# An own written order for the first four rounds of a software pipeline: a hybrid of convolution, attention and expert layers on one core

## The chip, the cores and the metric

The kernel runs on one NeuronCore of one Trainium2 chip. Its engines run side by side, each through its own list of instructions in order: TensorE (PE, matrix products into the eight PSUM banks), VectorE (DVE), ScalarE (ACT), GpSimd (POOL) and SyncE (SP, here only the issuer of loads and stores). They wait for each other through semaphores. The metric is the device time of one execution in microseconds (us), lower is better.

## The reference, cut to what matters

A batch of 16 images of 128 channels by 16 x 16 places goes through a dynamic convolution, an attention layer and a layer of eight experts. Only the first of these is touched in the rounds that the change rewrites; the other two follow it in the same pipeline.

```python
g = _gn(x)                                # mean and variance over groups of 4 channels of an image
key = softmax(K_w @ g + K_b)              # 49 rows of 256 places for each image
filters = g @ key.T                       # 128 channels x 49 taps
filters = conv0_w @ filters + conv0_b
filters = (filters - mean) * rsqrt(var + eps) * ln_w + ln_b
filters = conv1_w @ relu(filters) + conv1_b
x = x + depthwise_conv(g, filters)        # 7 x 7, an own filter for each image and channel
t = to_tokens(x)
t = t + attention(layernorm(t))           # softmax(tanh tanh'), 256 tokens of an image
t = t + experts(layernorm(t))             # 8 experts, the best 2 of each token
```

## The kernel before, in words

The 16 images are worked on as eight pairs. A loop over rounds, `for i in range(rounds)`, stands once in the list of each engine; in round `i` the pair `i` is in stage n (group normalisation), pair `i - 1` in stage a (keys and raw filter), `i - 2` in stage b (filter and spectrum), `i - 3` in stage c (product in the spectrum and inverse), `i - 4` in d (attention) and later pairs further on (`stages`). So round 0 has stage n alone, round 1 n and a, and so on: the first four rounds fill the pipeline. The order inside a round is that in which the loop's body is written on each engine, the same body for full rounds and for those that are mostly empty.

- Stage n of pair n. DVE: `bn_stats` and `bn_aggr` of the image (`gn_raw`, `gn_mv`). PE: the averages over groups by the constant matrix `group_avg` (`gn_avg`, line L1294), into `bank_d1`. DVE: deviation, square, sum (`gn_dev`, L955; `gn_sq`; `gn_e2`). PE: a second average (L1307). DVE: `gn_var`. POOL: power -1/2 (`gn_rstd`). DVE: `gn_bias` (L985). ACT: the normalised image `gbuf` (L627), which raises `g_done`.
- Stage a. PE waits for `g_done`, then four transposes of `gbuf` (L1215) and the key products (L1220). DVE: maximum `kmax` (L900) and shift (L907, L910). ACT: `kexp` (L589). DVE: `krec`. ACT: `kprob` (L596). PE: transposes of `kprob` (L1288), and after ACT's copies `gt` and `pt` the raw filter (L1314).
- Stage b. PE: first convolution (L1156), mean (L1160), spectrum of the image (L1106), mean square (L1164), second convolution (L1169). Stage c. PE: spectrum of the filter (L1174); DVE: products into `zhat`; PE: inverse (`image`, L1189, into `bank_o`).
- Beside this, in rounds 1 to 8, the weights of one expert are multiplied out (`expert_weights`, PE L1199 into `bank_d0`; DVE `weight_bias` L686 and `low_part` L692, ACT `w_high`).
- `keep_busy(bank, count)` (PE L1101) issues `count` products whose result nobody reads; they stand at places where PE would otherwise wait. In rounds 0 to 4 there are 25 of them.

All constant matrices lie in one tile `const`, identity first, the averaging matrix second. PE's first instruction waits for `ld_c1` at 32, that is for the first four matrices and for `small`, which SP loads behind the first pair of images. `load_x(p)` loads pair p; SP issues pair 2 and later ones once `g_done` frees the buffer, between the reloads of the expert weights.

Of the kernel before, what the change touches and what calls it, by code (L numbers as in the profile page):

```python
# [74 lines left out]
def constants():  # L75
# [33 lines left out]
    return {"ident": ident, "group": group, "mean": mean, "before": before,  # L109
# [3 lines left out]
WIDTHS = {"ident": P, "group": P, "mean": P, "before": P, "fwd": CHUNKS * (2 * WIDE + BOTH),  # L113
# [13 lines left out]
def build(nc, a_in, out):  # L127
# [9 lines left out]
    with ctx:  # L137
# [123 lines left out]
        ld_c1 = sem("ld_c1")  # L261
# [77 lines left out]
        CC = 3  # L339

# [6 lines left out]
        def expert_in(i):  # L347
            return experts_through(i) - 1 if i in expert_rounds else None

# [5 lines left out]
        with nc.Block() as block:  # L355

            @block.sync
            def _(sp):
# [13 lines left out]
                sp.dma_start(const[:, 0:STARTS["fwd"]], a_in["const"][:, 0:STARTS["fwd"]]).then_inc(ld_c1, 16)  # L372
# [37 lines left out]
            def _(pool):  # L410
# [23 lines left out]
                for i in range(rounds):  # L434
# [3 lines left out]
                    if b is not None:  # L438
                        pool.wait_ge(fvar_done, b + 1)
                        pool.tensor_tensor(frstd[:, :], fvar[:, :], minus_half[:, 0:2], ALU.pow).then_inc(frstd_done, 1)  # L440
                    if f is not None:
                        dispatch(f, range(TILES // 2, TILES))
                    if n is not None:
                        pool.wait_ge(gn_var_done, n + 1)
                        after(pool, g_done, n - 1)
                        pool.tensor_tensor(gn_rstd[:, n % 2, :], gn_var[:, :], minus_half[:, 0:2], ALU.pow).then_inc(gn_rstd_done, 1)  # L446
                    if c is not None:
                        pool.wait_ge(ln_var_done, c + 1)
                        after(pool, z_done, c)
                        pool.tensor_tensor(ln_rstd[:, :], ln_var[:, :], minus_half[:, :], ALU.pow).then_inc(ln_rstd_done, 1)  # L450
# [9 lines left out]

                def image_power(c):
                    pool.wait_ge(ln_var_done, c + 1)
                    pool.wait_ge(z_done, c)
                    pool.tensor_tensor(ln_rstd[:, :], ln_var[:, :], minus_half[:, :], ALU.pow).then_inc(ln_rstd_done, 1)
# [11 lines left out]
                pool.wait_ge(fvar_done, PAIRS)  # L476
                pool.tensor_tensor(frstd[:, :], fvar[:, :], minus_half[:, 0:2], ALU.pow).then_inc(frstd_done, 1)
# [26 lines left out]
            def _(act):  # L504
                act.dma_start(b1c[:, :], a_in["b1c"]).then_inc(ld_bias, 16)
# [6 lines left out]
                act.wait_ge(ld_c1, 32)  # L512
# [55 lines left out]
                for i in range(rounds):  # L568
                    n, a, b, c, d, e, _ = stages(i)
                    x = expert_in(i)  # L570
                    if a is not None:

                        act.wait_ge(gt_psum, a + 1)
                        after(act, fraw_psum, a - 1)
                        after(act, ghat_psum, 2 * (a - 1))
                        act.activation(gt[:, a % 2, :, :].rearrange("p h c -> p (h c)"), bank_t[:, :], ACT.Copy).then_inc(gt_done, 1)
# [8 lines left out]
                    if a is not None:  # L585

                        act.wait_ge(kshift_done, a + 1)
                        after(act, kprob_done, a)
                        act.activation(kexp[:, :], bank_k[:, 0:HW], ACT.Exp, bias=kshift[:, 0:1], accum_out=ktot[:, 0:1]).then_inc(kexp_done, 1)  # L589
# [3 lines left out]
                    if a is not None:  # L593
                        act.wait_ge(krec_done, a + 1)
                        after(act, pt_psum, a)
                        act.activation(kprob[:, :], kexp[:, :], ACT.Copy, scale=krec[:, 0:1]).then_inc(kprob_done, 1)  # L596
                    if x is not None and b is None and a is not None:

                        act.wait_ge(wbias_done, x + 1)
                        act.activation(w_high[:, x * 2 * HID:(x + 1) * 2 * HID], bank_d0[:, :], ACT.Copy).then_inc(whigh_done, 1)  # L600
# [5 lines left out]
                    if a is not None:  # L606

                        act.wait_ge(pt_psum, a + 1)
                        after(act, fraw_psum, a)
                        act.activation(pt[:, :, :].rearrange("p h k -> p (h k)"), bank_k[:, HW:2 * HW], ACT.Copy).then_inc(pt_done, 1)  # L610
                    if x is not None and b is not None and a is not None:

                        act.wait_ge(wbias_done, x + 1)
                        act.activation(w_high[:, x * 2 * HID:(x + 1) * 2 * HID], bank_d0[:, :], ACT.Copy).then_inc(whigh_done, 1)
                    if a is not None:

                        act.wait_ge(fraw_psum, a + 1)
                        after(act, conv0_psum, a - 1)
                        act.activation(fraw[:, a % 2, :, :], bank_k[:, 0:2 * KKP].rearrange("p (s k) -> p s k", s=2)[:, :, 0:KK],
                                       ACT.Copy).then_inc(fraw_done, 1)  # L620
                    if n is not None:

                        act.wait_ge(gn_bias_done, n + 1)
# [31 lines left out]
            def _(dve):  # L655
# [227 lines left out]
                for i in range(rounds):  # L883
# [41 lines left out]
                    if n is not None and i != 1:  # L925
                        image_statistics(n)
# [964 lines left out]
```

## Time and profile before

| | |
|---|---|
| median of 3 runs | 331.99 us (330.51 to 332.82) |
| the profiled execution | 332.61 us |
| its span, first to last instruction | 330.6 us |
| PE busy in the span | 294.9 us (89%) |
| granted clock of PE, mean | 0.974 |

Times in the trace count from the first instruction of the span; the execution's own time is 2.0 us longer. PE's busy time counts the products of `keep_busy` as well. A product of fp32 operands shows in the trace as two matmul records, a transpose as one, and the end of a record is modelled, so that lengths below are taken from one group's start to the next group's start.

### The profile page before, as it was taken

The page shows a single profiled execution, that of the slowest core. Times are in us where ns is not written, and L with a number is a line of the kernel's source. Part 1 is how long each engine was busy: PE and PEld are TensorE (multiplying, and loading weights), DVE is VectorE, ACT ScalarE, POOL GpSimd, SP SyncE. Part 2 cuts the span into 40 slices and gives each one's busy share as a digit, 9 for nine tenths or more (in the row PEclk, how much of TensorE's full clock was granted, in tenths as well). Part 3 has the DMA queues.
Part 4 walks back from the last instruction along what each step waited for, and adds up shares of the span by engine and source line. Part 5 has one row for each costly group of instructions (what it writes and reads, how often), then busy time and mean ns, then how long its engine had stood idle before and what let it go on. Part 6 is the DMA issues. An engine that isn't in the chain of part 4 may idle for free.

```text
span 330.6 us, 7149 instructions
## 1 busy us (share of the span) xinstructions
PE 294.9 (89%) x1739; PEld 237.7 (72%) x1739; DVE 231.7 (70%) x1012; ACT 144.2 (44%) x465; POOL 164.8 (50%) x187
## 2 busy tenths in 40 slices
PE   0889999999999999999998988996999999999910
PEld 0557677788777787778876765885888888888810
DVE  1524374679788797877889796784776677776883
ACT  1244343625337252371520324662666666666600
POOL 3000002021163656636747775775677777676650
PEclk9979999999999999999999999997999999999985
DMA  7751423050211810001101113433333234325946
GB/s 206 261 175 29 149 70 108 0 161 14 82 48 29 287 44 25 25 18 42 34 25 50 43 41 92 107 113 95 105 98 102 83 100 114 97 79 149 332 160 249
DMA packets 29919, 33.39 MB, mean 101 GB/s; under 512 B 5064, under 2 KB 23836, under 8 KB 29626
## 3 DMA queue, kind: packets, MB, share of 16 engines
q1 hardware_dynamic: 24608, 23.64, 24.3%
q0 software_dynamic: 4352, 8.60, 7.6%
q10 hardware_dynamic: 922, 0.71, 0.6%
q8 instruction: 16, 0.26, 0.3%
q14 instruction: 21, 0.17, 0.2%
HBM read 21.69 MB, written 11.68 MB: 101 GB/s over the span
## 4 chain that ended last, share of the span: by engine, by line
PE 63%; DVE 10%; issue 7%; SPq 6%; DMA 5%; POOL 5%; ACT 2%; DVEq 0%; POOLq 0%; ACTq 0%
PE bank L1821 7%; PE bank L1189 6%; PE bank L1106 6%; PE bank L1199 4%; PE bank L1801 4%; PE bank L1796 4%; PE bank L1797 4%; PE bank L1810 4%; PE bank L1174 3%; PE bank L1181 3%; POOL rows_dram L429 3%; PE bank L1101 3%; SPq L1560 2%; SPq L1557 2%; PE bank L1791 2%
## 5 line engine op out<-in xcount | busy, mean ns | idle before, releaser
L1505 POOL DMA_INDIRECT moe_dram<-ys,xs x71 | 70.0, 987 | 28.7 <-issue 18.8
L429 POOL DMA_INDIRECT rows_dram<-row,slot x56 | 55.7, 994 | 24.6 <-issue 13.5
L1821 PE MATMUL bank<-w_all,gatedt 128*128 x284 | 44.1, 278 | 0.1
L1593 ACT ACTIVATE silu<-bank 128x256 f32<-128x256 f32 x71 | 27.3, 384 | 31.6 <-PE bank L1801 31.6
L1736 DVE SCALAR_TENSOR_TENSOR ys<-b_all,xs,bank 128x128 f32<-128x128 f32 x71 | 24.7, 348 | 22.6 <-issue 20.7
L1753 DVE SCALAR_TENSOR_TENSOR gated<-bank,xs,silu 128x256 f32<-128x256 f32 x71 | 34.3, 482 | 7.1 <-ACT silu L1593 2.7
L1821 PEld LDWEIGHTS bank<-w_all,gatedt 128*128 128x128 f32 x284 | 37.7, 193 | 0.3 <-issue 0.3
L1796 PE MATMUL bank<-w_high,x_high 128*128 x71 | 34.4, 485 | 0.7 <-ACT x_high L1580 0.7
L440 POOL TENSOR_TENSOR frstd<-fvar,minus_half 128x2 f32<-128x2 f32 x7 | 5.0, 707 | 52.4 <-DVE fvar L812 52.4
L1189 PE MATMUL bank<-zhat,const 121*128 121x256 f32 (+1 forms) x128 | 29.6, 383 | 0.1
L1801 PE MATMUL bank<-w_high,x_low 128*128 x71 | 28.9, 407 | 0.2
L1797 PE MATMUL bank<-w_low,x_high 128*128 x71 | 28.1, 396 | 0.0
L1810 PE MATMUL bank<-const,gated 128*128 128x128 f32 x142 | 27.4, 275 | 0.6 <-DVE gated L1753 0.6
L1584 ACT ACTIVATE gatedt<-bank 128x256 f32<-128x256 f32 x71 | 26.8, 378 | 1.2 <-PE bank L1810 1.1
L1810 PEld LDWEIGHTS bank<-const,gated 128*128 128x128 f32 x142 | 19.7, 141 | 9.5 <-DVE gated L1753 1.4
L1189 PEld LDWEIGHTS bank<-zhat,const 121*128 121x128 f32 (+1 forms) x128 | 23.6, 189 | 3.7 <-issue 0.5
L1580 ACT ACTIVATE x_high<-bank 128x128 fp32r<-128x128 f32 x71 | 19.7, 278 | 13.0 <-PE bank L1791 6.0
L1101 PE MATMUL bank<-const 128*128 128x256 f32 x88 | 25.2, 416 | 0.0
L1727 DVE TENSOR_TENSOR x_low<-bank,x_high 128x128 fp32r<-128x128 f32 x71 | 20.1, 283 | 5.1 <-ACT x_high L1580 4.9
L1106 PE MATMUL bank<-gt,const 128*121 128x256 f32 (+1 forms) x96 | 22.8, 385 | 0.0
L1791 PE MATMUL bank<-const,xs 128*128 128x128 f32 x71 | 19.6, 278 | 3.0 <-DMA xs<-rows_dram 2.9
L446 POOL TENSOR_TENSOR gn_rstd<-gn_var,minus_half 128x2 f32<-128x2 f32 x8 | 5.7, 715 | 32.5 <-DVE gn_var L976 32.4
(203 smaller groups left out, 617.1 us busy)
## 6 DMA issues: line engine op xcount, KB each, us to landing
xs<-rows_dram SPq DMA_DIRECT2D x71, 66.0 KB, 1.9
xc<-in_x SPq DMA_DIRECT2D x8, 256.0 KB, 2.8
wgv<-in_wg SPq DMA_DIRECT2D x8, 256.0 KB, 2.8
wgv<-in_wv SPq DMA_DIRECT2D x8, 256.0 KB, 3.1
xt<-in_xt SPq DMA_DIRECT2D x4, 512.0 KB, 4.7
xt<-moe_dram SPq DMA_DIRECT2D x8, 256.0 KB, 4.2
moe_dram<-ys,xs POOLq DMA_INDIRECT x71, 2.4
const<-in_const SPq DMA_DIRECT2D x1, 1123.0 KB, 9.1
```

Of the source, the lines that this page charges most:

```text
L429: pool.indirect_dma_start(rows_dram, bass.IndirectOffsetOnAxis(ap=slot[:, f % 2, 2 * t + k:2 * t + k + 1], axis=0), row[:, f % 2, t, k, :] ...
L1101: pe.matmul(bank, ident, const[:, 0:2 * P], start=True, stop=True)
L1106: last = pe.matmul(bank_s[r // 2][0:tile_rows[r], r % 2 * 2 * C:(r % 2 + 1) * 2 * C], fwd[:, h, tile_cols[r]], gt[:, b % 2, h, :], start=( ...
L1189: last = pe.matmul(bank_o[:, h * 2 * C:(h + 1) * 2 * C], inv[0:tile_rows[r], r, h * P:(h + 1) * P], zhat[0:tile_rows[r], r, :], start=(r = ...
L1505: pool.indirect_dma_start(moe_dram, bass.IndirectOffsetOnAxis(ap=xs[:, u, C + 1:C + 2].bitcast(U32), axis=0), ys[:, u, :], None, bounds_ch ...
L1593: act.activation(silu[:, j % 2, :], bank_h[j % 2][:, 0:HID], ACT.Silu).then_inc(S["silu_done"], 1)
L1753: dve.scalar_tensor_tensor(gated[:, j % 2, :], bank_h[j % 2][:, HID:2 * HID], xs[:, j % U, C:C + 1], silu[:, j % 2, :], ALU.mult, ALU.mult ...
L1796: pe.matmul(bank_h[j % 2][:, :], x_high[:, j % 2, :], w_high[:, bass.ds(e * (2 * HID), 2 * HID)], start=True, stop=False)
L1797: pe.matmul(bank_h[j % 2][:, :], x_high[:, j % 2, :], w_low[:, bass.ds(e * (2 * HID), 2 * HID)], start=False, stop=False)
L1801: pe.matmul(bank_h[j % 2][:, :], x_low[:, j % 2, :], w_high[:, bass.ds(e * (2 * HID), 2 * HID)], start=False, stop=True).then_inc(S["h_psu ...
L1810: last = pe.transpose(bank_g[:, h * P:(h + 1) * P], gated[:, j % 2, h * P:(h + 1) * P], ident)
L1821: last = pe.matmul(bank_y[j % 2][:, 0:C], gatedt[:, j % 2, h * P:(h + 1) * P], w2_all[:, bass.ds(e * (2 * C) + h * C, C)], start=(h == 0), ...
```

## The change

The first four rounds are no longer run by the loop. Each engine has them written out as a list of calls (`HEAD = 4`; the loops begin at `HEAD`), and the bodies of the loop become small functions that the lists and the loop share. In the lists, on PE, DVE, ACT and POOL alike, the statistics of the next pair stand earlier: `image_statistics(n + 1)` and `group_statistics(n + 1)` behind the bias of pair n, the first average right behind the key products, the deviation right behind the key shift, the second average in the middle of the round. For these four pairs the averages go to `bank_o` and not to `bank_d1` (`group_places`). The averaging matrix comes first in `const` and is loaded by itself, from ACT's queue (`ld_group`); PE starts with it and waits for the other constants after the first pair's averages. `router_weights` (the router's constants) moves from round 1 to round 3. Of the 25 products of `keep_busy` four are left.

```diff
-    return {"ident": ident, "group": group, "mean": mean, "before": before,
+    return {"group": group, "ident": ident, "mean": mean, "before": before,
...
+        def group_places(n):
+
+            return bank_o if n < HEAD else bank_d1, slice(0, 2), slice(4, 6)
...
                 load_x(0)
-                sp.dma_start(const[:, 0:STARTS["fwd"]], a_in["const"][:, 0:STARTS["fwd"]]).then_inc(ld_c1, 16)
+                sp.dma_start(const[:, P:STARTS["fwd"]], a_in["const"][:, P:STARTS["fwd"]]).then_inc(ld_c1, 16)
...
             def _(act):
+                act.dma_start(const[:, 0:P], a_in["const"][:, 0:P]).then_inc(ld_group, 16)
                 act.dma_start(b1c[:, :], a_in["b1c"]).then_inc(ld_bias, 16)
...
+                image_copy(1)
+                first_conv(0)
+                key_exp(1)
+                key_prob(1)
+                wide_spectrum(0)
+                squares(0)
+                rest_spectrum(0)
+                key_copy(1)
+                normalised_image(2)
+                filter_copy(1)
+                expert_copy(1)
...
+                group_power(0)
+                group_power(1)
+                group_power(2)
+                filter_power(0)
+                group_power(3)
+                filter_power(1)
+                image_power(0)
...
+                image_statistics(0)
+                group_statistics(0)
+                group_deviation(0)
+                group_moment(0)
+                group_variance(0)
+                image_statistics(1)
+                group_statistics(1)
+                group_bias(0)
+                bias_columns()
+                weight_differences(0)
...
+                key_max(1)
+                key_shift(1)
+                group_deviation(2)
+                group_moment(2)
+                key_reciprocal(1)
+                centred(0)
+                scaled(0)
+                group_variance(2)
...
-                pe.wait_ge(ld_c1, 32)
-
...
+                pe.wait_ge(ld_group, 16)
+                group_mean(0)
+                group_square(0)
+                pe.wait_ge(ld_c1, 32)
+                pe.wait_ge(ld_bias, 32)
+                pe.transpose(bank_b[0:EXPERTS * 4, 0:P], bgv[:, :], ident).then_inc(bgt_psum, 1)
+                keep_busy(bank_t[:, 0:2 * P], 2)
+
+                image_transpose(0)
+                keys(0)
+                pe.wait_ge(gn_var_done, 1)
+                group_mean(1)
+                expert_weights(1, 0)
+                group_square(1)
+                key_transpose(0)
+                keep_busy(bank_d1[:, 0:2 * P], 1)
+                raw_filter(0)
+                keep_busy(bank_t[:, 0:2 * P], 1)
+
+                image_transpose(1)
...
+                image_transpose(2)
+                keys(2)
+                pe.wait_ge(filt_done, 1)
+                first_conv(1)
+                pe.wait_ge(gn_var_done, 3)
+                group_mean(3)
+                pe.wait_ge(wlow_done, 2)
+                filter_spectrum(0, 0)
+                filter_spectrum(0, 1)
+                filter_mean(1)
+                group_square(3)
+                pe.wait_ge(ghat_done, 2)
+                features_spectrum(1, (0, 1))
+                key_transpose(2)
+                features_spectrum(1, (2,))
+                filter_square(1)
+                expert_weights(3, 2)
+                pe.wait_ge(gn_var_done, 4)
+                image(0)
+                raw_filter(2)
+                filter_of(1)
+
+                for i in range(HEAD, rounds):
...
-                        if a < 4:
-                            keep_busy(bank_t[:, 0:2 * P], (3, 2, 2, 4)[a])
...
-                        if b < 2:
-                            keep_busy(bank_o[:, 0:2 * P], 3)
...
-                        if c is None:
-                            keep_busy(bank_o[:, 0:2 * P], (0, 1, 5)[i])
```

What this does to the order is seen at three places. In the rows below `bank7` is `bank_d1`, `bank3` is `bank_o`, and `x4` is four equal instructions in a row.

PE at the start, before: the first product needs all that `ld_c1` counts; three idle products stand ahead of the first transposes.

```order
L1294 MATMUL bank7<-gn_mv,const 128x2
L1307 MATMUL bank7<-gn_e2,const 128x2
L1326 MATMUL bank2<-const,bgv 32x128
L1101 MATMUL bank1<-const 128x256 x3
L1215 MATMUL bank1<-const,gbuf 128x128 x4
L1220 MATMUL bank0<-gbuf,small 64x256 x2
```

PE at the start, now.

```order
L1384 MATMUL bank3<-gn_mv,const 128x2
L1389 MATMUL bank3<-gn_e2,const 128x2
L1396 MATMUL bank2<-const,bgv 32x128
L1250 MATMUL bank1<-const 128x256 x2
L1356 MATMUL bank1<-const,gbuf 128x128 x4
L1363 MATMUL bank0<-gbuf,small 64x256 x2
L1384 MATMUL bank3<-gn_mv,const 128x2
L1348 MATMUL bank6<-wgv,w1d 128x512 x2
L1389 MATMUL bank3<-gn_e2,const 128x2
```

The first two products no longer share a wait with the rest, and the averages of pair 1 (the second L1384 and L1389) now stand right behind the first pair's keys.

PE from the expert weights of round 2 to the transposes of pair 2, before: both averages of the next pair stand behind the round's long products.

```order
L1199 MATMUL bank6<-wgv,w1d 128x512 x2
L1288 MATMUL bank0<-const,kprob 128x128 x2
L1294 MATMUL bank7<-gn_mv,const 128x2
L1101 MATMUL bank3<-const 128x256 x5
L1307 MATMUL bank7<-gn_e2,const 128x2
L1314 MATMUL bank0<-pt,gt 128x64 x4
L1169 MATMUL bank2<-small,frelu 49x128 x2
L1101 MATMUL bank1<-const 128x256 x2
L1215 MATMUL bank1<-const,gbuf 128x128 x4
```

PE from the first average of pair 2 to the transposes of pair 2, now.

```order
L1384 MATMUL bank3<-gn_mv,const 128x2
L1255 MATMUL bank4<-gt,const 121x256 x4
L1309 MATMUL bank2<-fsum,const 128x2
L1389 MATMUL bank3<-gn_e2,const 128x2
L1255 MATMUL bank5<-gt,const 124x256 x2
L1369 MATMUL bank0<-const,kprob 128x128 x2
L1313 MATMUL bank2<-fsqs,const 128x2
L1348 MATMUL bank6<-wgv,w1d 128x512 x2
L1377 MATMUL bank0<-pt,gt 128x64 x4
L1318 MATMUL bank2<-small,frelu 49x128 x2
L1356 MATMUL bank1<-const,gbuf 128x128 x4
```

The first average stands ahead of the spectrum, the second ahead of the spectrum's last part, the key transposes and the weights, and no idle product is left between them.

DVE in the same round, before: the deviation `gn_dev` of the next pair stands behind the two long steps on the expert weights.

```order
L812 TENSOR_SCALAR fvar<-bank2 128x2
L686 TENSOR_TENSOR bank6<-bank6,bg_row 1x512
L692 TENSOR_TENSOR w_low<-bank6,w_high 128x512
L955 TENSOR_TENSOR gn_dev<-gn_mv,bank7 128x2
L956 COPY gn_mean<-bank7 128x2
L958 TENSOR_TENSOR gn_sq<-gn_dev 128x2
L963 TENSOR_TENSOR gn_e2<-gn_sq,gn_mv 128x2
L818 SCALAR_TENSOR_TENSOR fln<-flw,frstd,small 128x49 x2
L823 TENSOR_SCALAR frelu<-fln 128x98
L976 TENSOR_SCALAR gn_var<-bank7 128x2
L985 SCALAR_TENSOR_TENSOR gn_bias<-gn_mean,gn_rstd 128x2
```

DVE in the same round, now.

```order
L947 TENSOR_REDUCE kmax<-bank0 128x1
L951 TENSOR_TENSOR ksum_b<-kmax,small 128x1
L954 TENSOR_TENSOR kshift<-small,ksum_b 128x1
L969 TENSOR_TENSOR gn_dev<-gn_mv,bank3 128x2
L970 COPY gn_mean<-bank3 128x2
L972 TENSOR_TENSOR gn_sq<-gn_dev 128x2
L976 TENSOR_TENSOR gn_e2<-gn_sq,gn_mv 128x2
L958 RECIPROCAL krec<-ktot 128x1
L866 TENSOR_TENSOR fcen<-f0,bank2 128x98
L870 TENSOR_TENSOR flw<-fcen,small 128x98
L982 TENSOR_SCALAR gn_var<-bank3 128x2
L874 TENSOR_SCALAR fvar<-bank2 128x2
```

The four short steps on the groups moved from behind the weights to right behind the key shift.

## Rows read from the trace of the kernel before

**Rows 1.** Windows of round 3, of round 4, and of a stretch in round 1.

```profile
core 0: us, PE busy (x) PEld busy (x) DVE busy (x) ACT busy (x) POOL busy (x), PEclk, DMA share, GB/s
36.62:53.82 17.20, 17.20 (x86) 13.30 (x86) 9.84 (x40) 5.99 (x19) 2.40 (x3) 1.00 0.29 88
53.82:72.68 18.86, 18.26 (x102) 14.37 (x101) 10.92 (x46) 8.04 (x28) 2.40 (x3) 1.00 0.25 77
19.80:23.10 3.30, 3.30 (x14) 2.18 (x12) 0.57 (x3) 1.77 (x4) 0.17 (x1) 0.50 0.49 162
```

**Rows 2.** Timeline of PE at the start: start, length, line, records, wait before.

```profile
7.59 0.59 PE L1294 MATMUL bank<-gn_mv,const 128*128 128x2 f32 x2 [7.59 <-DMA small<-in_small]
9.44 2.77 PE L1101 MATMUL bank<-const 128*128 128x256 f32 x6
12.00 1.06 PE L1215 MATMUL bank<-const,gbuf 128*128 128x128 f32 x4
12.99 0.65 PE L1220 MATMUL bank<-gbuf,small 128*64 128x256 f32 x4
```

**Rows 3.** Timeline of PE in round 3, from the transposes of pair 2.

```profile
36.62 0.65 PE L1215 MATMUL bank<-const,gbuf 128*128 128x128 f32 x4
...
37.79 0.46 PE L1156 MATMUL bank<-fraw,small 128*128 128x98 f32 x2
38.19 1.99 PE L1174 MATMUL bank<-filt,const 49*121 49x256 f32 x8
40.10 0.38 PE L1160 MATMUL bank<-fsum,const 128*128 128x2 f32 x2
40.34 2.83 PE L1106 MATMUL bank<-gt,const 128*121 128x256 f32 x12
43.01 1.46 PE L1101 MATMUL bank<-const 128*128 128x256 f32 x6
44.31 0.28 PE L1164 MATMUL bank<-fsqs,const 128*128 128x2 f32 x2
44.45 1.96 PE L1199 MATMUL bank<-wgv,w1d 128*128 128x512 f32 x4
46.25 0.38 PE L1288 MATMUL bank<-const,kprob 128*128 128x128 f32 x2
...
46.61 3.71 PE L1189 MATMUL bank<-zhat,const 121*128 121x256 f32 x16
50.15 0.28 PE L1307 MATMUL bank<-gn_e,const 128*128 128x2 f32 x2
...
51.31 0.64 PE L1169 MATMUL bank<-small,frelu 128*49 128x128 f32 x4
51.88 1.99 PE L1101 MATMUL bank<-const 128*128 128x256 f32 x8
```

**Rows 4.** Timeline of DVE: the first pair's statistics, steps of rounds 2 and 3.

```profile
3.73 0.75 DVE L880 BATCH_NORM_STATS2 gn_raw<-xc 128x6 f32<-128x256 f32 x2 [2.72 <-DMA xc<-in_x]
4.52 0.25 DVE L939 BATCH_NORM_AGGREGATE gn_mv<-gn_raw 128x2 f32<-128x6 f32 x2
...
32.96 0.15 DVE L955 TENSOR_TENSOR gn_dev<-gn_mv,bank 128x2 f32<-128x2 f32 x1
...
40.69 0.42 DVE L900 TENSOR_REDUCE kmax<-bank 128x1 f32<-128x256 f32 x1
```

**Rows 5.** Timeline of ACT in rounds 2 and 3.

```profile
35.48 1.09 ACT L627 ACTIVATE gbuf<-xc,gn_bias,gn_rstd 128x256 f32<-128x256 f32 x2 [0.31 <-DVE gn_bias L985]
...
43.95 0.46 ACT L589 ACTIVATE kexp<-bank,kshift 128x256 f32<-128x256 f32 x1
...
44.73 0.51 ACT L596 ACTIVATE kprob<-kexp,krec 128x256 f32<-128x256 f32 x1 [0.23 <-DVE krec L922]
```

**Rows 6.** Load of pair 1, issued at 2.2 us: the tile's view in that stretch.

```profile
L360 SPq DMA_DIRECT2D xc<-in_x x1: 434/434/434, 2.2 to 2.2; - x1
...
DMA to landing us min/median/max: 6.3/6.3/6.3
```

More of the change, by code:

```diff
@@ new lines, in normalised_image @@
+                def normalised_image(n):
+                    act.wait_ge(gn_bias_done, n + 1)
+                    after(act, keys_done, n - 1)
+                    after(act, gt_psum, n - 1)
+                    for s in range(2):
+                        last = act.activation(gbuf[:, n % 2, s * HW:(s + 1) * HW], xc[:, n % 2, s * HW:(s + 1) * HW], ACT.Identity,
+                                              scale=gn_rstd[:, n % 2, s:s + 1], bias=gn_bias[:, n % 2, s:s + 1])
+                    last.then_inc(g_done, 1)
@@ L593, in _ @@
                     if a is not None:
[L594 to L600, printed above, removed]
+                        key_prob(a)
                     if d is not None:
@@ L606, in _ @@
                     if a is not None:
[L608 to L614, printed above, removed]
+                        key_copy(a)
+                    if x is not None and a is not None:
+                        expert_copy(x)
                     if a is not None:
[L617 to L620, printed above, removed]
+                        filter_copy(a)
                     if n is not None:
[L623 to L629 removed]
+                        normalised_image(n)
                 first_conv(7)
@@ new lines, in _ @@
+                filter_variance(0)
+                group_bias(2)
+                normalised(0)
+                rectified(0)
+                weight_bias(1)
+                image_statistics(3)
+                group_statistics(3)
+                filter_of(0)
+                low_part(1)
+                weight_differences(2)
+                key_max(2)
+                key_shift(2)
+                group_deviation(3)
+                group_moment(3)
+                products(0)
+                key_reciprocal(2)
@@ new lines, in _ @@
+                centred(1)
+                scaled(1)
+                spectrum(0)
+                group_variance(3)
+                rest_products(0)
+                filter_variance(1)
+                group_bias(3)
+                normalised(1)
+                rectified(1)
+                weight_bias(2)
+                router_weights()
+                low_part(2)
+                image_sum(0)
+                image_stats(0)
+                filter_of(1)
+                z_of(0)
+                weight_differences(3)
@@ L1200, in expert_weights, with image_transpose @@
                     last.then_inc(wmul_psum, 1)
-                for i in range(rounds):
+                def image_transpose(a):
+                    after(pe, gt_done, a)
+                    pe.wait_ge(g_done, a + 1)
+                    for h in range(CHUNKS):
+                        for s in range(2):
+                            last = pe.transpose(bank_t[:, h * 2 * C + s * C:h * 2 * C + (s + 1) * C],
+                                                gbuf[:, a % 2, s * HW + h * P:s * HW + (h + 1) * P], ident)
+                    last.then_inc(gt_psum, 1)
@@ new lines, in keys, with key_transpose @@
+                def keys(a):
+                    after(pe, fraw_done, a)
+                    for s in range(2):
+                        last = pe.matmul(bank_k[s * KKP:(s + 1) * KKP, 0:HW], kw_t, gbuf[:, a % 2, s * HW:(s + 1) * HW], start=True, stop=True)
+                    last.then_inc(keys_done, 1)
+                def key_transpose(a):
+                    pe.wait_ge(kprob_done, a + 1)
+                    for h in range(CHUNKS):
+                        last = pe.transpose(bank_k[:, HW + h * P:HW + (h + 1) * P], kprob[:, h * P:(h + 1) * P], ident)
+                    last.then_inc(pt_psum, 1)
@@ new lines, in _ @@
+                filter_spectrum(0, 1)
[10 more added lines that the diff above has]
+                raw_filter(2)
+                filter_of(1)
+                for i in range(HEAD, rounds):
```

289 lines of the change are left out of this document (175 added, 114 removed).

## The prediction

> **What bounds the kernel now.** I looked first at the busy shares (TensorE 89% of the span), then at windows cut at the transposes that open each round, then at PE's timeline inside one such window. In rounds 3 and 4 PE is busy 17.20 of 17.20 us and 18.26 of 18.86 us [rows 1], so PE's list sets the pace and the other engines have room (DVE 9.84 and 10.92). But a full PE is not a useful PE: inside round 3 the six records at 43.01 and the eight at 51.88 are idle products [rows 3], 1.30 us to the square at 44.31 and 1.94 us to the transposes at 53.82 that open the next window [rows 1]. They stand there because the next real product is not ready. So the head of the program is bound by chains across engines, and PE merely hides the waits. The clearest chain is the group normalisation of the next pair: the deviation starts at 32.96 [rows 4], and the transposes that need its image start at 36.62 [rows 3], 3.66 us later. The other chain is the softmax of the keys, with the maximum (0.42) [rows 4], two short steps, exponential and probability (43.95 to 45.24) [rows 5], at least 1.7 us of work. At the very start PE's first product waits until 7.59 for `small` [rows 2], though the first pair's statistics are ready at 4.77 [rows 4].
>
> The number to compare is therefore the start of the transposes of pair 3: 53.82 before. They stand 41.82 after those of pair 0, at 12.00 [rows 2].
>
> **How much of that is real work.** From start to start in round 3 [rows 3]: 36.62 to 43.01 is 6.39, 44.31 to 51.88 is 7.57, together 13.96 without idle products. Round 2 of the changed program (between pair 2 and pair 3) has all of it. The round between pairs 1 and 2 lacks the filter spectrum (38.19 to 40.10, 1.91) and the inverse (46.61 to 50.15, 3.54): 8.51. The round between pairs 0 and 1 also lacks the first convolution (37.79 to 38.19, 0.40), the mean (0.24), the image's spectrum (40.34 to 43.01, 2.67), the square (0.14) and the second convolution (51.31 to 51.88, 0.57): 4.49. That sums to 26.96. One idle product is 1.30/3 = 0.43; two of the four that are left lie in this stretch: 0.86. So PE has 27.82 us to do at full clock. Of the 41.82 before, 22 idle products (25 less the three ahead of the first transposes) are 9.5, and 41.82 - 26.96 - 9.5 = 5.4 are open waits and work at the low clock.
>
> **Idle products removed.** Alone this is worth nothing: their place was a wait. It pays only if the chains are covered by real work, which the new order has to supply. Twenty of them, 8.6 us, go from the stretch.
>
> **Averages sooner.** The chain of 3.66 now starts behind the key products of the round and not behind the weights. Between the first average and the next transposes PE has in a full round the spectrum 2.67, the mean 0.24, the square 0.14, the expert weights and key transposes (44.45 to 46.61, 2.16), the second average and raw filter (50.15 to 51.31, 1.16) and the second convolution 0.57 [rows 3]: 6.9 us without the inverse. It covers the chain almost twice. DVE gains nothing else: the same four short steps (0.15 us for the deviation [rows 4]) move past two long ones. In front of them DVE now waits for PE's average directly; behind that wait are the key reciprocal and `centred`, needed by the raw filter and the square, both later on PE by more than a microsecond. The other bank for the averages removes a sharing with the expert weights' side of PSUM and has no time of its own; it is what allows the place. The key chain is covered in a full round by first convolution, mean and spectrum (3.3 to 3.6). In the first round it isn't: between the keys and the key transposes there are only the two averages (0.3) and the expert weights 1.80 (44.45 to 46.25) [rows 3], 2.1 against 1.7 and four passages between engines. I put down 0.4 for such open hand-offs. The bounds are 0 and 3.66, one whole group chain left open; I stand near the low end because only the first round has a cover as short as its chain.
>
> **The start.** The matrix by itself comes on ACT's queue, so the first average no longer waits for `small` at 7.59. What is late next is DVE: `image_statistics(1)` now stands ahead of `group_bias(0)`, and it waits for the load of pair 1, issued at 2.2 with 6.3 to landing [rows 6], 8.5. Statistics and aggregate take 3.73 to 4.77, 1.04 [rows 4]; the bias about as long as one of DVE's short steps (0.15); `gbuf` 1.09 [rows 5]. 8.5 + 1.04 + 0.15 + 1.09 = 10.8, against 12.00. [...] Bounds: 12.0, rival A; and 9.2, if pair 1 lands in time and the old chain (7.59 to 12.00, 4.41) simply begins at 4.77.
>
> **The clock.** [...] It rose after work without a break from 9.44. It was low again at 19.80 to 23.10 (0.50) [rows 1]. In the new order less stands ahead of the first transposes, and round 0 has short waits in it, so work between transposes is done at the low clock that was not before. [...]
>
> **The sum.** 10.8 + 27.8 + 2.6 + 0.4 = 41.6 for the transposes of pair 3, against 53.82: 12.2 earlier. Round 4 stays as it is (18.86, PE 97% busy), being the loop's body as before, apart from what lies ahead of it; the later rounds start from each other, so the shift runs to the end. The profiled execution took 332.61 with 2.0 of it around the span, 0.6 over the median of 331.99; minus 12.2 is 320.4, and on the median **319.8 us**.
>
> **Rivals.** (A) *The matrix comes no earlier.* It shares the way from memory with the load of pair 0, which lands at 3.73 [rows 4], and with others that let `small` land only at 7.59 [rows 2]; it may come anywhere between. At 7.59 the whole old chain remains (7.59 to 12.00) and only the head's start is lost, 1.2: 321.0. [...] The trace of before doesn't tell which, since its first product waited for all of those loads at once. I keep the early one, because the pair's own load, issued beside the matrix and four times as large (256 places of two images against 128 columns), is there at 3.73 [rows 4]. Chance of A 0.12.
>
> (B) *One chain stays open in the written order.* Lists on five engines written by hand can leave one hand-off in a round where two engines wait for each other in turn: one chain of 3.66 in full, 319.8 + 3.7 = 323.5. For it: before, even the filled rounds had 5.4 of waits and low clock; against it: covers of 6.9 and 3.3. Chance 0.12.
>
> (C) *The shift is given back.* If rounds 4 to 8 were paced by something that doesn't move with PE (the reloads of the expert weights on SP, say), the transposes of pair 3 would come at 41.6 and a later round would swallow it: 332. Against it: PE is 97% busy in round 4 [rows 1]; a round with so little slack has no room to swallow 12 us, though eight rounds with 0.6 each could hide that a load is just in time. Chance 0.05.
>
> (D) *Slower: the clock stays low.* The idle products also kept PE busy. [...] The relapse at 19.80 [rows 1] shows that the clock does fall in this head. Against it: the list now has real work without a break where the idle products stood. [...] Chance 0.04.
>
> **How the numbers follow.** My forecast has 0.67. Its own range: 1.5 less at the low clock, 0.4 less of waits and 0.5 of the start's 1.6 give 317.4; 2.6 more at the low clock give 322.4. With A inside that and B at 323.5, the range 317.4 to 323.8 leaves out C, D and the tails of two bad terms at once, some 0.15. Within 1% (about what a measurement of this kernel can tell from no change) is 328.7 to 335.3: C and a sum of several misses, 0.06. Slower by over 1%: D, 0.04. Faster: 0.90.
>
> **What would show it.** Right: the first average near 5, transposes of pair 0 near 10.8, of pair 3 near 41.6, PE full from 11 to 41 with half-rate records only in the first round, the rounds from pair 3 on as long as before (18.9 for the first). `gn_dev` right behind `kshift`, and PE not waiting for `g_done`. Wrong: A shows in the first average past 7; B in one gap of over 2 us on PE between transposes; C in equal starts before pair 8; D in records of double length past 25. The likeliest error is the clock's term, then the start.

## The result, and the profile after

The changed kernel takes 319.82 us (median of 4 runs, 318.26 to 320.27) against 332.4 for the kernel before beside it; the ratio is 0.964, 95% interval 0.9597 to 0.9684. Its profiled execution took 319.43, 13.2 less than the one before. A second set of runs of the same kernel gave 320.54 (ratio 0.9666, 0.9631 to 0.9701). Medians and ratios are of fast runs: one of the six runs with the bias first, at 320.96, was slow and is left out.

From here on, and in the expectations but for the old bank's, round k opens with the transposes of pair k; the loop's own count, by which the windows of [rows 1] are rounds 3 and 4, is one higher. The timeline of PE in the changed kernel (start, length, line, records, wait before) shows where each round opens, the lines L1356:

```profile
5.22 0.56 PE L1384 MATMUL bank<-gn_mv,const 128*128 128x2 f32 x2 [5.22 <-DVE gn_mv L963]
...
10.99 1.12 PE L1356 MATMUL bank<-const,gbuf 128*128 128x128 f32 x4 [2.04 <-ACT gbuf L620]
12.04 1.12 PE L1363 MATMUL bank<-gbuf,small 128*64 128x256 f32 x4
13.09 0.59 PE L1384 MATMUL bank<-gn_mv,const 128*128 128x2 f32 x2
13.54 3.06 PE L1348 MATMUL bank<-wgv,w1d 128*128 128x512 f32 x4
16.43 0.28 PE L1389 MATMUL bank<-gn_e,const 128*128 128x2 f32 x2
...
16.82 0.60 PE L1250 MATMUL bank<-const 128*128 128x256 f32 x2
17.46 1.10 PE L1377 MATMUL bank<-pt,gt 128*128 128x64 f32 x8
18.40 0.65 PE L1250 MATMUL bank<-const 128*128 128x256 f32 x2
19.16 0.63 PE L1356 MATMUL bank<-const,gbuf 128*128 128x128 f32 x4
...
27.54 0.66 PE L1356 MATMUL bank<-const,gbuf 128*128 128x128 f32 x4
...
41.41 0.66 PE L1356 MATMUL bank<-const,gbuf 128*128 128x128 f32 x4
...
60.40 0.63 PE L1356 MATMUL bank<-const,gbuf 128*128 128x128 f32 x4
```

Pair 3 opens at 41.41, 12.41 earlier than before, and pair 4 at 60.40, 12.28 earlier than the end of the window in [rows 1]. From there every round starts 12.28 earlier, up to the last pair (122.10 against 134.38). The rest of the 13.2 lies in the tail, whose code is the same; with pair 7 opening at 122.03, another execution of the changed kernel took 1.3 less than this one. So the start of pair 3 measures the change better than the total does.

The windows between these starts (columns as in [rows 1]; the clock column misses the low spell of round 0, which the lengths of the records show):

```profile
10.99:19.16 8.17, 8.02 (x31) 4.62 (x31) 3.65 (x17) 3.29 (x9) 0.71 (x1) 1.00 0.62 206
19.16:27.54 8.38, 8.38 (x49) 6.21 (x49) 5.12 (x22) 5.99 (x20) 1.39 (x2) 1.00 0.46 135
27.54:41.41 13.87, 13.87 (x73) 10.71 (x72) 10.01 (x39) 6.16 (x20) 1.40 (x2) 1.00 0.55 166
41.41:60.40 18.99, 18.33 (x102) 14.37 (x101) 12.22 (x54) 8.04 (x28) 3.41 (x4) 1.00 0.28 92
```

Rounds 1 and 2 are full of real work, with no idle product in them. The round that opens at 41.41 is as long as it was (18.99; 18.86 before).

DVE at the start, its deviation and bias of pair 3, and ACT's images of pairs 0 to 3:

```profile
8.73 0.75 DVE L942 BATCH_NORM_STATS2 gn_raw<-xc 128x6 f32<-128x256 f32 x2 [1.53 <-DMA xc<-in_x]
...
9.68 0.13 DVE L987 SCALAR_TENSOR_TENSOR gn_bias<-gn_mean,gn_rstd 128x2 f32<-128x2 f32 x1
...
29.79 0.15 DVE L969 TENSOR_TENSOR gn_dev<-gn_mv,bank 128x2 f32<-128x2 f32 x1
...
34.92 0.16 DVE L987 SCALAR_TENSOR_TENSOR gn_bias<-gn_mean,gn_rstd 128x2 f32<-128x2 f32 x1
```

```profile
9.85 1.09 ACT L620 ACTIVATE gbuf<-xc,gn_bias,gn_rstd 128x256 f32<-128x256 f32 x2 [4.90 <-DVE gn_bias L987]
...
17.92 1.09 ACT L620 ACTIVATE gbuf<-xc,gn_bias,gn_rstd 128x256 f32<-128x256 f32 x2 [0.52 <-DVE gn_bias L987]
...
24.69 1.09 ACT L620 ACTIVATE gbuf<-xc,gn_bias,gn_rstd 128x256 f32<-128x256 f32 x2
...
35.26 1.09 ACT L620 ACTIVATE gbuf<-xc,gn_bias,gn_rstd 128x256 f32<-128x256 f32 x2
```

The first bias waits in line behind the statistics of pair 1, which wait for its load. ACT made the image of pair 3 in the kernel before at

```profile
52.68 1.09 ACT L627 ACTIVATE gbuf<-xc,gn_bias,gn_rstd 128x256 f32<-128x256 f32 x2 [1.01 <-DVE gn_bias L985]
```

so that it was ready at 53.77, and PE took it at 53.82. Now it is ready at 36.35 and PE takes it at 41.41: a chain that in the old place ended just as PE needed it has 5 us to spare. Pair 2 has 1.8 (25.78 to 27.54), pair 1 hardly any (19.01 to 19.16).

### The profile page after: what moved, and what is told of

Read it like the earlier page. It is cut to its first block, busy times and chain, and to the rows that moved or that the text cites. A ratio compares the mean times of both kernels' runs of the same rounds, so it can differ in the third digit from the quotient of the medians.

```text
span 317.6 us, 7079 instructions
## 1 busy us (share of the span) xinstructions
PE 285.4 (90%) x1697; PEld 229.8 (72%) x1697; DVE 232.0 (73%) x1012; ACT 143.8 (45%) x465; POOL 164.9 (52%) x187
## 4 chain that ended last, share of the span: by engine, by line
PE 65%; DVE 11%; issue 7%; DMA 6%; POOL 4%; SPq 3%; ACT 2%; DVEq 1%; POOLq 0%; ACTq 0%
PE bank L2024 7%; PE bank L1338 7%; PE bank L1255 6%; PE bank L1348 5%; PE bank L1999 4%; PE bank L2004 4%; PE bank L2000 4%; PE bank L2013 4%; PE bank L1323 4%; PE bank L1330 3%; POOL rows_dram L434 3%; PE bank L1994 2%; DMA xc<-in_x 2%; PE bank L1292 2%; DVE ln_raw L724 2%
## 5 line engine op out<-in xcount | busy, mean ns | idle before, releaser
L1338 PE MATMUL bank<-zhat,const 121*128 121x256 f32 (+1 forms) x128 | 29.5, 383 | 0.1
L1338 PEld LDWEIGHTS bank<-zhat,const 121*128 121x128 f32 (+1 forms) x128 | 23.7, 189 | 4.1 <-issue 1.0
L441 POOL TENSOR_TENSOR frstd<-fvar,minus_half 128x2 f32<-128x2 f32 x8 | 5.7, 710 | 30.5 <-DVE fvar L874 30.4
L1255 PEld LDWEIGHTS bank<-gt,const 128*121 128x121 f32 (+1 forms) x96 | 17.0, 185 | 2.3
```

Of the source, the lines that this page charges most:

```text
L1255: last = pe.matmul(bank_s[r // 2][0:tile_rows[r], r % 2 * 2 * C:(r % 2 + 1) * 2 * C], fwd[:, h, tile_cols[r]], gt[:, b % 2, h, :], start=( ...
L1338: last = pe.matmul(bank_o[:, h * 2 * C:(h + 1) * 2 * C], inv[0:tile_rows[r], r, h * P:(h + 1) * P], zhat[0:tile_rows[r], r, :], start=(r = ...
```

## The experiments

The theory: real work now stands where the group chain runs, so the idle products that covered it can go; the start is a smaller term of its own. The rivals: the idle products were needless anyway; or the start does it all; or the bank. The move of `router_weights` has no run of its own.

**Idle products out of the old order.** In the kernel before, the 22 behind the first transposes are removed:

```diff
-                        if a < 4:
-                            keep_busy(bank_t[:, 0:2 * P], (3, 2, 2, 4)[a])
+                        if a < 1:
+                            keep_busy(bank_t[:, 0:2 * P], 3)
...
-                        if b < 2:
-                            keep_busy(bank_o[:, 0:2 * P], 3)
...
-                        if c is None:
-                            keep_busy(bank_o[:, 0:2 * P], (0, 1, 5)[i])
```

> The kernel before without the 22 idle products that stand behind the first transposes; all else as before. Theory (the idle products covered waits, the chains between the engines set the pace): nothing is won. The transposes of pair 3 stay near 53.8 us or come later, up to 60, because PE now idles at those places and its clock may fall again; time 332 to 339 us. Rival (the idle products themselves were on the path and the new order only got rid of them): pair 3 at 53.8 - 9.5 = 44.3, time 322.9 us.

Measured: 342.79 us, ratio 1.0317 (1.0267 to 1.0367), slower even than the theory's range, and 20 us away from the rival. The window of PE from the transposes of pair 0 to those of pair 3, and PE at the end of round 1:

```profile
12.08:62.16 50.08, 38.87 (x147) 26.64 (x147) 19.72 (x83) 15.71 (x47) 4.50 (x6) 0.76 0.31 94
```

```profile
33.94 0.28 PE L1288 MATMUL bank<-gn_mv,const 128*128 128x2 f32 x2
36.47 0.38 PE L1299 MATMUL bank<-gn_e,const 128*128 128x2 f32 x2 [2.25 <-DVE gn_e L963]
...
39.70 1.08 PE L1215 MATMUL bank<-const,gbuf 128*128 128x128 f32 x4 [0.39 <-ACT gbuf L627]
```

PE is idle for 50.08 - 38.87 = 11.2 us, and the 26.96 us of real work take 38.87, 11.9 more than at full clock (a little less at the low clock itself, since the modelled end of a record ahead of a wait counts as busy). The same stretch in the kernel before:

```profile
12.00:53.82 41.82, 39.88 (x191) 28.84 (x190) 19.62 (x83) 15.83 (x47) 4.50 (x6) 0.96 0.38 114
```

It had 1.9 us of waits and, beside 26.96 of real work and 9.5 of idle products, 3.4 of such excess. So the idle products became waits (9.3 more), as the theory says; and the clock fell (0.76 over the stretch against 0.96), which made the excess 8.5 larger: nearly as much again.

**Idle products into the new order.** Twenty are put back where they stood, for instance

```diff
                 features_spectrum(0, (2,))
                 key_transpose(1)
+                keep_busy(bank_t[:, 0:2 * P], 3)
                 filter_square(0)
...
                 filter_mean(1)
+                pe.wait_ge(gt_done, 3)
+                keep_busy(bank_t[:, 0:2 * P], 5)
                 group_square(3)
```

> The changed kernel with 20 idle products put back at the places where the kernel before had them, in the new order. Theory (real work now covers the chains, so an idle product only adds its own length): 20 x 0.43 = 8.6 us more, pair 3's transposes at about 50.0 instead of 41.4, time 328.4 us, at least 327. Rival (PE still waits at those places, and the products would lie in the waits): pair 3 at 41.4 to 43, time 320 to 321 us.

Measured: 327.87 us, ratio 0.9884 (0.9826 to 0.9942). Pair 3 opens at 50.51; PE is busy without a break:

```profile
10.55:50.51 39.96, 39.96 (x190) 29.91 (x191) 20.33 (x84) 15.54 (x47) 4.33 (x6) 1.00 0.46 143
```

The theory holds. The two runs and the two kernels make a table:

| | with the idle products | without |
|---|---|---|
| order of before | 332.0 | 342.8 |
| written order | 327.9 | 319.8 |

Taking idle products out (22 in the upper row, 20 in the lower) costs 10.8 in one order and wins 8.1 in the other.

**Averages back at their old places.** The changed kernel with the two averages of pairs 1 to 3, and the steps that hang on them on DVE, ACT and POOL, where the loop has them, and in their old bank. The key transposes go back behind the weights with them. PE in round 2:

```diff
-                group_mean(3)
...
-                group_square(3)
...
-                key_transpose(2)
...
                 expert_weights(3, 2)
-                pe.wait_ge(gn_var_done, 4)
+                key_transpose(2)
+                pe.wait_ge(zhat_done, 2)
+                group_mean(3)
                 image(0)
+                group_square(3)
```

> The changed kernel, its early start and its few idle products kept, but the two averages of pairs 1 to 3 back at their old places on PE, DVE, ACT and POOL, and in their old bank. Theory (the place of the averages is what covers the chain): the group chain lies open in each of three rounds, 3 to 4 us each, and PE's clock falls in the gaps: pair 3's transposes at 51 to 54, time 330 to 333 us, about all of the gain gone. Rival (the few idle products and the start make the gain, places don't matter): pair 3 at 41.4 to 43, time 320 to 321 us.

Measured: 338.76 us, ratio 1.021 (1.0158 to 1.0263): all of the gain is gone, and more. PE at the end of the round that opens at 23.85, and the windows from pair 0 to pair 3:

```profile
33.52 0.28 PE L1384 MATMUL bank<-gn_mv,const 128*128 128x2 f32 x2
36.05 0.38 PE L1389 MATMUL bank<-gn_e,const 128*128 128x2 f32 x2 [2.25 <-DVE gn_e L976]
...
39.04 1.08 PE L1356 MATMUL bank<-const,gbuf 128*128 128x128 f32 x4 [0.39 <-ACT gbuf L620]
```

```profile
11.36:23.85 12.49, 9.79 (x31) 5.84 (x31) 4.31 (x18) 3.88 (x9) 0.71 (x1) 0.84 0.59 182
23.85:39.04 15.19, 12.55 (x49) 8.59 (x49) 5.41 (x23) 5.88 (x19) 1.39 (x2) 0.72 0.28 89
39.04:59.48 20.44, 19.52 (x72) 14.16 (x73) 8.59 (x32) 6.07 (x19) 1.39 (x2) 0.72 0.26 77
```

The waits are only 48.12 - 41.86 = 6.3 us (the three lengths less PE's busy time); 41.86 busy for 27.82 of work is 14.0 more than at full clock, against 2.4 in the changed kernel. The longest wait in each of the first two rounds, 2.25 (at 19.53 and 36.05), ends on `gn_e`, so it is the averages' chain and not the key transposes. The place of the averages carries the gain. My expectation had 3 to 4 us of waits in each of the three rounds: there are 2.7, 2.6 and 0.9, since in the third the inverse (L1338) still stands between the two averages. It had the clock's part too small.

**The matrix late.** The changed kernel with the averaging matrix in the common load, PE's first wait as before:

```diff
-                act.dma_start(const[:, 0:P], a_in["const"][:, 0:P]).then_inc(ld_group, 16)
...
-                pe.wait_ge(ld_group, 16)
+                pe.wait_ge(ld_c1, 32)
                 group_mean(0)
```

> The changed kernel with the averaging matrix back in the common load of constants, for which PE's first product waits. Theory (the start is a term of its own, carried to the end): first average at 7.6, first transposes at 12.2 instead of 11.0, pair 3 at 42.5, time 320.8 to 321.8 us. Rival (the start is hidden, because the second pair's load paces round 0 anyway): first transposes later, but pair 3 at 41.4 and the time unchanged at 319.8 us.

Measured: 319.7 us, ratio 0.9641 (0.96 to 0.9681), the same as the changed kernel. In the trace

```profile
7.18 0.58 PE L1383 MATMUL bank<-gn_mv,const 128*128 128x2 f32 x2 [7.18 <-DMA small<-in_small]
...
11.41 1.11 PE L1355 MATMUL bank<-const,gbuf 128*128 128x128 f32 x4 [0.48 <-ACT gbuf L619]
...
42.65 0.66 PE L1355 MATMUL bank<-const,gbuf 128*128 128x128 f32 x4
```

the first average is 2 us later, but the first transposes only 0.42, and pair 3 by 1.24 (0.8 of it a longer round 0: 8.98 against 8.17). Against a second profile of the changed kernel, which opens pair 0 at 10.46 and pair 3 at 41.34 with a round 0 of 8.63, it is 0.95 and 1.31. The total doesn't show what the profiles do; its interval, 1.3 us to either side, is as wide as the step, so it settles neither side by itself.

**Bias first.** On DVE the first pair's bias ahead of the second pair's statistics; beside it, on the same chip, the changed kernel again:

```diff
+                group_bias(0)
                 image_statistics(1)
                 group_statistics(1)
-                group_bias(0)
                 bias_columns()
```

> The changed kernel once more, as the yardstick of this set: 319.8 us, transposes of pair 0 at 11.0, of pair 3 at 41.4.

> The changed kernel with the first pair's bias ahead of the second pair's statistics on DVE, so that it no longer stands behind the wait for that pair's load. Theory (the start is bound by that wait, and what is won there is carried to the end): first transposes at 9.6 instead of 11.0, the clock rises sooner as well, pair 3 at 38.9 to 39.7, time 317.4 to 318.2 us. Rival (round 0 is paced by the second pair's own load, so the wait only moves to its averages): pair 3 at 41 or more, 319.8 us.

Measured: 320.54 (0.9666, 0.9631 to 0.9701) for the changed kernel and 317.41 (0.9577, 0.9533 to 0.9621) with the bias first; the intervals just don't meet. The first transposes stand at 9.54 and pair 3 at 40.12, 1.2 earlier than the 41.34 beside it; the profiles show no more of the 3.1 between the medians. The theory holds in its direction, with less from the clock than I had put down (round 0 still takes 8.3, and pair 3 misses the 38.9 to 39.7).

**Both.** Bias first, and the matrix late:

> The changed kernel with the first pair's bias ahead of the second pair's statistics, and the averaging matrix back in the common load. Theory (the earlier load of the matrix is worth little in the changed kernel only because the bias stands behind the second pair's load): the first transposes at 11.4 to 12.3, where the late matrix alone had 11.4, so the 2 us of the two steps together are lost, pair 3 at 42.0 to 43.2, time 319.7 to 321.5 us. Rival (the bias's place alone makes the earlier start): first transposes at 9.6, pair 3 at 40.1, time 317.6 us.

Measured: 320.18 us, ratio 0.9634 (0.9597 to 0.9671); first transposes at 12.10, pair 3 at 43.34. So with the bias first the early matrix is worth 1.9 us by the ratios (0.9634 against 0.9577, from two sets of runs, whose intervals meet) and 3.2 at pair 3's start, and without it nothing that the total shows. Up to 0.7 of the 3.2 is this execution's own: `small` lets the first average start at 7.90 here and at 7.18 in the run before. Whichever of two waits ends last hides the other: with the matrix late, the bias comes 2.9 us behind the first average in either order (10.11 after 7.18; 10.76 after 7.90).

**More and fewer idle products at the start.** Four instead of two ahead of the first transposes, and none of the four in the head:

```diff
-                keep_busy(bank_t[:, 0:2 * P], 2)
+                keep_busy(bank_t[:, 0:2 * P], 4)
```

> The changed kernel with four idle products instead of two ahead of the first transposes; they fill the 2.0 us in which PE waits for the first normalised image. Theory (the low clock in round 0 is a term of about 2 us, and an unbroken start ends it sooner): first transposes at 11.0 to 11.4, the expert weights of round 0 at full rate, pair 3 at 39.7 to 40.6, time 318.0 to 319.0 us. Rival (the clock's rise doesn't hang on this gap): pair 3 at 41.4 to 41.8, time 319.8 to 320.2 us.

> The changed kernel without its last four idle products. Theory (what is left of them keeps the clock, and covers two short waits in round 0): no gain from the 0.9 us of work removed; the clock rises later or falls again in round 0 or 1, pair 3 at 41.4 to 42.7, time 319.8 to 321.1 us. Rival (idle products are only work): pair 3 at 40.5, time 318.9 us.

Measured: 319.95 (0.9615, 0.9563 to 0.9666) and 320.32 us (0.9657, 0.9624 to 0.9691), both the same as the changed kernel beside them. The second is as the theory said: pair 3 at 42.02, and the products' time is now waits of 0.47 and 0.34 in round 0. The first doesn't test what it should: pair 1's load landed late in its profiled execution (its statistics begin at 9.85, against 8.73), so that PE still waited 1.38 ahead of transposes at 12.10. It shows that four idle products with that gap behind them don't bring the rise: the weights of round 0 take 3.56.

**Bias first and three idle products**, which close the gap that was left:

```diff
-                keep_busy(bank_t[:, 0:2 * P], 2)
+                keep_busy(bank_t[:, 0:2 * P], 3)
```

> The changed kernel with the first pair's bias ahead of the second pair's statistics, and three idle products instead of two, which close the gap of 0.44 us that is left ahead of the first transposes. Theory (what holds the clock low in round 0 are gaps ahead of the first transposes): first transposes at 10.0 to 10.4, full rate from the expert weights of round 0 on, round 0 of 7 us, pair 3 at 39.2, 1 us earlier than without the third product, time 316.7 us. Rival (the clock rises some 5 to 7 us after the first transposes, whatever stands ahead of them): round 0 still 8.3 to 9, pair 3 at 40.5 to 41, time 318.0 to 318.5 us.

Measured: 316.79 us, ratio 0.9548 (0.9511 to 0.9585), the fastest version; its interval meets that of bias first alone, not that of the changed kernel. PE at its start:

```profile
7.12 2.77 PE L1250 MATMUL bank<-const 128*128 128x256 f32 x6
9.68 1.06 PE L1356 MATMUL bank<-const,gbuf 128*128 128x128 f32 x4
10.67 1.12 PE L1363 MATMUL bank<-gbuf,small 128*64 128x256 f32 x4
11.72 0.46 PE L1384 MATMUL bank<-gn_mv,const 128*128 128x2 f32 x2
12.04 1.96 PE L1348 MATMUL bank<-wgv,w1d 128*128 128x512 f32 x4
13.84 0.28 PE L1389 MATMUL bank<-gn_e,const 128*128 128x2 f32 x2
...
17.54 0.63 PE L1356 MATMUL bank<-const,gbuf 128*128 128x128 f32 x4 [0.93 <-ACT gbuf L620]
```

The weights of round 0 (12.04 to 13.84) run at full rate, 1.80 against 3.05 with bias first alone, so the theory on the clock holds; but pair 3 stands at 39.80, only 0.32 earlier than with bias first alone. PE now waits 0.93 for the image of pair 1 at the end of round 0: it is faster there than that pair's chain.

**The start alone.** The kernel before with only the matrix first and loaded by itself, and PE's first wait split:

> The kernel before with the start of the changed one alone: the averaging matrix first in the tile and loaded by itself, PE's first wait split; orders and idle products as before. Theory (the chains of rounds 1 to 3 follow each other, so an earlier first round moves all of them): first transposes at 9.8 to 10.4 instead of 12.0, pair 3 at 52 to 52.6, time 330.2 to 330.8 us. Rival (the loads of the second pair and of the first expert pace round 0): pair 3 at 53.5 to 53.8, time 331.5 to 332 us.

Measured: 330.67 us, ratio 0.996 (0.9931 to 0.999). First transposes at 9.80, pair 3 at 51.74, 2.1 earlier than before; the theory holds, and the start is a small part of the change.

**The old bank.** The changed kernel with the averages in `bank_d1`, which puts a wait and a later second average into round 2 (the window before the transposes of pair 3):

```diff
-            return bank_o if n < HEAD else bank_d1, slice(0, 2), slice(4, 6)
+            return bank_d1, slice(0, 2), slice(4, 6)
...
                 filter_spectrum(0, 0)
+                pe.wait_ge(gn_e2_done, 4)
                 filter_spectrum(0, 1)
```

> The changed kernel with the averages of the first four pairs in the old bank again. In round 3 the filter's spectrum fills that bank, so there PE waits for DVE's read of the first average ahead of the spectrum's second half, and the second average, its variance and its power move behind the products. Theory (the bank has no time of its own, it only allows the place): rounds 0 to 2 as before, pair 3 0 to 1 us later (41.4 to 42.4), time 319.8 to 320.8 us. Rival (sharing the bank with the spectrum is itself a cost in every round): the transposes of pairs 1 and 2 late as well, over 2 us in all, 322 us or more.

Measured: 320.89 us, ratio 0.965 (0.9608 to 0.9692). The rounds between its transposes (12.84, 21.22, 29.59 and 44.17) are 8.38, 8.37 and 14.58, against 8.17, 8.38 and 13.87: 0.7 in the round where the filter's spectrum needs the bank, nothing clear elsewhere. The start at 12.84 is pair 1's load again (statistics at 10.58). The expectation counts as the loop does, so this is its round 3. The bank has hardly a time of its own.

## Why the prediction was right, point by point

- **The bound.** PE's list set the pace, and chains stood under the idle products: shown by the table of the two orders.
- **The cover, 6.9 against 3.66.** Right in size: from the first average of pair 2 to its transposes are 6.94 (20.60 to 27.54). But the chain grew, because its second average stands in PE's list behind other work: 5.2 to the finished image (25.78), so that 1.8 was to spare instead of 3.3. The run with the averages back at their old places shows that the cover is what wins.
- **Real work, 27.82.** The stretch after is 41.41 - 10.99 = 30.42, of it 30.27 busy in the windows of the profile after. Less the low clock's share below, 27.9 is work: right to 0.1.
- **The clock, 2.6.** No run shows this term as it stands in the sum, nor the 1.5 less and 2.6 more of the range; what the runs show in its place is 2.3. In round 0 the transposes and keys take 2.10 (10.99 to 13.09) against 1.17 in [rows 3], the average 0.45 against 0.14, the weights 2.89 against 1.80: 0.93 + 0.31 + 1.09 = 2.3. The size held, in part by luck: I set it without knowing what decides it, and in the second profile of the changed kernel the same groups lose 2.8. What the runs show of it stands in the last section.
- **Open hand-offs, 0.4.** 30.42 - 27.82 - 2.3 = 0.3. They stand in round 0, where I had put them: 0.64 and 0.76 from two idle products to the next group, for 0.43 each, which makes 0.5.
- **The start, 10.8.** 10.99, and paced by pair 1's load, as I had it. But I gave the earlier start to the matrix, with 12.0 as the price of a late one (rival A). The late matrix gave 11.41, with `small` at 7.18: of the 1.2, about 0.4. The step was too coarse there; the same matrix is worth 1.9 by the ratios, and up to 3.2 at pair 3's start, once the bias doesn't stand behind the load. That 10.99 came so near was also luck: in the profiles with the changed kernel's start, bias in its place, pair 0 opens between 10.46 and 12.84, as that load lands. In every profile with the matrix on ACT's queue pair 0's own statistics begin at 4.04 to 4.25, against 3.73 in [rows 4] and 3.67 to 3.75 in the three others without it: that load comes 0.3 to 0.6 later beside the added one.
- **The rounds after.** 18.99 and then the same starts, 12.28 earlier: rival C is out. B has no place: no gap of over 2 us lies between the transposes.
- **The other bank.** I said that it ends a sharing with the weights' side. What shares `bank_d1` in the rewritten rounds is the filter's spectrum, and going back to it costs 0.7 in one round.
- **Idle products "alone worth nothing".** This is where I was wrong, though it has no term in the sum: alone, their removal costs 10.8. I had counted the wait that they covered and not the clock, which was 0.96 over the stretch with them and 0.76 without. Rival D, the low clock, is real in the old order: the excess of 11.9 us, 8.5 more than before, lies in the first experiment's stretch, and 3.3 more in the round behind it (22.13 from pair 3 to pair 4, 84.29 - 62.16, against 18.86). In the changed kernel PE has no wait from 19.16 to 41.41, and the records there run at full rate (granted clock 1.00).

The predicted 319.8 met the median to 0.02, which is luck: its own terms, or a repeat (320.54), can't hold as close.

## What to carry to other kernels

Idle products can mark where a chain is uncovered: move the chain's first step to right behind what it needs, so that real work covers it, and only then take them out, since taken out first they cost the wait and, here, the clock (9.3 us more of waits, and 8.5 more of work at the low clock). Look for what ends last at each wait before giving a term to a cause: the early matrix and the early bias were worth 2.5 us together at pair 3's start (42.65 to 40.12; 2.1 by the ratios), and apart the totals show nothing of either. In a pipeline whose rounds repeat, compare the start of the first full round: two executions of the changed kernel agree there to 0.07 us where their totals differ by 1.3. But it carries the landing of the first loads, so set it beside the start of pair 0 (43.28 behind a late load in the run with four idle products).

## What the runs showed of the hardware

An open wait on PE can cost more than its length: with the averages back at their old places 6.3 us of waits came with 14.0 us more busy time than at full clock, the granted clock being 0.84, 0.72 and 0.72 over its three rounds, with 0.50 from 24.00 to 30.00 and 1.00 from 52.00 to 59.40 (some 2.4 of the 14.0 at the start, where the changed kernel loses 2.3 as well). It need not: the start alone had 2.9 us of waits in its stretch (the longest 1.03) and ran at full rate from 12.33 on (granted clock 1.00 up to pair 3 at 51.74), and the kernel before, with 1.9, fell to 0.50 at 19.80 [rows 1]. What decides between them no run here shows.

The rise at the start hung on small gaps. Where idle products stand right up to the first transposes (the old order's start in three profiles, and three idle products with the bias first), the weights of round 0 take 1.8 us, the full rate. In all ten other profiles PE waits 0.44 to 3.84 us ahead of the transposes, and the same weights take 2.89 to 3.56. The pair that differs in one idle product shows it most plainly: a gap of 0.44 and weights of 3.05, no gap and 1.80. A gap later on didn't matter in the start alone: 0.41 between keys and weights, and the weights still took 1.82. In every profile the first four transposes run at the low rate, 1.06 to 1.12 against 0.66 in a full round; in the kernel before, four of them at 21.54 take 1.06 as well, where the granted clock was 0.50 [rows 1].

And pair 1's load, issued at 2.2 us, let its statistics begin between 8.20 and 10.58 us in the nine profiles in which DVE waits for it, which alone moves the changed kernel's first transposes by over 2 us (10.46 to 12.84).
